# The opening of a fused layer-norm and linear-attention kernel: two steps listed by hand on every engine, norms of the weights taken over partitions by TensorE

## The reference

```python
q = (x @ Wq.T).reshape(B, L, H, D)
k = (x @ Wk.T).reshape(B, L, H, D)
v = (x @ Wv.T).reshape(B, L, H, D)
phi_q = jax.nn.elu(q) + 1.0
phi_k = jax.nn.elu(k) + 1.0
...
S = S + pk_t[..., :, None] * v_t[..., None, :]
z = z + pk_t
num = jnp.einsum('bhd,bhde->bhe', pq_t, S)
den = jnp.sum(pq_t * z, axis=-1, keepdims=True) + EPS
...
return out @ Wo.T + bo
```

## Time and profile before

| what | value |
|---|---|
| median of 3 runs | 969.82 us (969.0 to 972.33) |
| the profiled execution | 969.87 us, its span 968.1 us |
| busy share of the span | PE 93%, DVE 85%, ACT 78%, POOL 74% |
| mean granted clock of PE | 0.97 |

### The profile page before, as it was taken

One profiled execution on the slowest core, in us unless ns is written; L12 is line 12 of the kernel. 1 busy time (PEld: TensorE's weight loads), 2 busy tenths in 40 slices (PEclk: granted clock), 3 DMA queues, 4 the chain that ended last, 5 costly groups with the idle time before them and its releaser, 6 DMA issues. The chain is left out here.

```text
span 968.1 us, 29903 instructions
## 1 busy us (share of the span) xinstructions
PE 898.7 (93%) x10240; PEld 524.6 (54%) x10240; DVE 825.5 (85%) x1513; ACT 759.3 (78%) x1327; POOL 713.2 (74%) x879
## 2 busy tenths in 40 slices
PE   1368999999999999999999999999999999999974
PEld 1134555565555556655555556555555566555541
DVE  3376899998999999999999999999999999988763
ACT  4457888887888888888888888888888888878761
POOL 1036778777977777788877877788777777888761
PEclk8589999999999999999999999999999999999996
DMA  7136688787666877676767776776678776777772
GB/s 261 31 66 122 121 174 156 159 141 144 150 147 150 173 152 161 141 150 147 153 145 163 164 161 147 139 155 147 150 150 173 152 160 142 149 125 128 130 129 65
DMA packets 421404, 139.80 MB, mean 144 GB/s; under 512 B 402544, under 2 KB 402544, under 8 KB 421360
## 3 DMA queue, kind: packets, MB, share of 16 engines
q1 hardware_dynamic: 404496, 106.73, 59.4%
q10 hardware_dynamic: 16864, 32.51, 10.2%
HBM read 21.76 MB, written 16.78 MB: 40 GB/s over the span
## 5 line engine op out<-in xcount | busy, mean ns | idle before, releaser
L1125 PE MATMUL PJ<-wT,XT 128*128 128x512 f16 x2304 | 530.0, 382 | 15.4 <-DMA XT<-XH 7.6
L1125 PEld LDWEIGHTS PJ<-wT,XT 128*128 128x128 f16 x2304 | 217.7, 98 | 264.4 <-issue 18.0
L454 POOL TENSOR_TENSOR A<-AM,A 128x512 f16<-128x512 f32 x256 | 292.4, 1162 | 33.0 <-ACT A L649 33.0
L1224 PE MATMUL PJ<-wT,AT 128*128 128x512 f16 x768 | 178.5, 382 | 1.7 <-DMA AT<-ATTN 1.5
L446 POOL TENSOR_SCALAR_AFFINE_SELECT AM<-AM 128x512 f32<-128x512 f32 x128 | 81.8, 639 | 117.7 <-ACT AM L639 117.5
L649 ACT ACTIVATE A<-AM 128x512 f16<-128x512 f32 x256 | 153.9, 630 | 10.6 <-POOL AM L446 10.5
L1195 PE MATMUL AV<-SS,QS 128*128 128x33 f16 x1024 | 112.2, 178 | 5.4 <-POOL A L454 4.4
L1198 PE MATMUL AV<-VN,A 128*128 128x33 f16 x3072 | 116.9, 178 | 0.0
L1224 PEld LDWEIGHTS PJ<-wT,AT 128*128 128x128 f16 x768 | 71.7, 98 | 80.1 <-DMA AT<-ATTN 2.8
L1198 PEld LDWEIGHTS AV<-VN,A 128*128 128x128 f16 x3072 | 109.3, 96 | 3.7
L891 DVE TENSOR_TENSOR AM<-SC,causal 128x512 f32<-128x512 f32 x128 | 87.6, 684 | 22.9 <-PE SC L1175 22.7
(11 more groups left out here) (98 smaller groups left out, 1522.9 us busy)
## 6 DMA issues: line engine op xcount, KB each, us to landing
out_dram<-Y ACTq DMA_DIRECT2D x32, 512.0 KB, 3.1
X<-in_L_attn_x_dram ACTq DMA_DIRECT2D x30, 512.0 KB, 3.5
X<-in_L_attn_x_dram SPq DMA_DIRECT2D x2, 512.0 KB, 7.2
A<-in_L_attn_Wk_dram SPq DMA_DIRECT2D x1, 1024.0 KB, 9.4
A<-in_L_attn_Wq_dram SPq DMA_DIRECT2D x1, 1024.0 KB, 11.7
QS<-in_L_attn_Wv_dram SPq DMA_DIRECT2D x1, 1024.0 KB, 13.8
QS<-in_L_attn_Wo_dram SPq DMA_DIRECT2D x1, 1024.0 KB, 15.8
XT<-XH SPq DMA_TRANSPOSE x64, 3.5
```

The lines of the kernel that those rows point to most:

```text
L454: g.tensor_tensor(A[:, b, LO, hg], AM[:, k % 4], A[:, b, HI, hg], ALU.subtract).then_inc(a_lo.sem, 1)
L1125: ins = t_.matmul(PJ[b], XT[:, w, c, b * C:(b + 1) * C], wT[m_][:, m, c, :], start=(c, w, m) == todo[0], stop=(c, w, m) == todo[-1])
L1224: ins = t_.matmul(PJ[b], AT[:, b, w, c * C:(c + 1) * C], wT[3][:, m, c, :], start=(c, w, m) == todo[0], stop=(c, w, m) == todo[-1])
```

## The change

The loop and the end of the kernel keep their operations and their order. What is changed lies before step 1:

1. Every engine gets a function `opening()` that lists the preparation, step -1 and step 0 together, one operation a line; `run` begins at step 1. In it the squares, turned blocks and halves of the weights stand singly (a quarter of a weight at a time) between the operations of the chunks.
2. The maximum over partitions is no longer POOL's. For each weight PE turns the column of 128 partial maxima into one row (`turn_norm`), DVE reduces the row (`top_norm`), PE spreads the one number to all partitions by a matmul with a row of ones (`spread_norm`), and DVE makes the scale from it (`scale_w`, three linked instructions). The square root becomes a shift of the exponent bits by one place. The other scales come in `scale_rest`.
3. `gain` and `shift` have a semaphore each. DVE waits for the gain alone ahead of the first statistics and halves the shift after them (`half_gain`, `half_shift`). POOL and PE no longer wait for `zeroed`.
4. `NORMS` takes one of the PSUM banks, so that three spare banks serve the turned blocks instead of four; `W_REUSE` is 5 instead of 6.
5. `turn_q` waits in its first two steps for the high halves (`wT_hi`) of the weights that lie in the memory it writes.
6. The helper `wait(...)` becomes `wait_ge(*signal.upto(...))`, with the same counts.

```diff
-        W_BANKS = PJ + (SC + [AV2[:, i] for i in range(2)]) * 3 + SC
-        W_REUSE = len(PJ + SC) + 2
+        NORMS = AV2[:, 0]
+        spare = [SC[0], SC[1], AV2[:, 1]]
+        W_BANKS = PJ + [spare[k % 3] for k in range(4 * GROUPS - 2)]
+        W_REUSE = len(PJ + spare)
...
-            for s in range(-1, 4):
+            for s in range(1, 4):
...
+                        else:
+                            sp.wait_ge(wT_hi, (4 if ATTEND else 3) * GROUPS)
...
-            pool.wait_ge(zeroed, 1)
...
-                g.partition_all_reduce(norm2_all[:, at], norm2[:, at], P, RMAX).then_inc(norm2_reduced, 1)
-                pool.wait_ge(norm2_reduced, pair + 1)
-                g.tensor_tensor(norm[:, at], norm2_all[:, at], half4[:, at], ALU.pow).then_inc(norm_done, 1)
...
+            def row_sums(j):
+
+                m = W_ORDER[j]
+                dve.wait_ge(w_summed, (j + 1) * GROUPS)
+                link(v.tensor_reduce(norm2[:, m:m + 1], sumsq[:, m], mybir.AxisListType.X, ALU.max))
+                v.tensor_scalar(norm2[:, m:m + 1], norm2[:, m:m + 1], 1e-30, None, ALU.max).then_inc(norm2_done, 1)
+
+            def top_norm(j):
+
+                dve.wait_ge(norm_turned, j + 1)
+                v.tensor_reduce(norm_max[:, j:j + 1], NORMS[0:1, j * P:(j + 1) * P], mybir.AxisListType.X, ALU.max).then_inc(norm_max_done, 1)
+
+            def scale_w(j):
...
+                link(v.tensor_scalar(pow2[:, at].bitcast(U32), NORMS[:, j * P:j * P + 1].bitcast(U32), 1, EXP_BITS,
+                                     ALU.logical_shift_right, ALU.bitwise_and))
                 link(v.reciprocal(rpow2[:, at], pow2[:, at]))
...
+                v.tensor_scalar(w_scale[:, at], rpow2[:, at], TOP / HALF_EXP, None, ALU.mult).then_inc(w_scaled, 1)
+                dve.wait_ge(w_scaled, j + 1)
...
+            def turn_norm(j):
+
+                m = W_ORDER[j]
+                pe.wait_ge(norm2_done, j + 1)
+                t_.transpose(NORMS[0:1, j * P:(j + 1) * P], norm2[:, m:m + 1], ident[:]).then_inc(norm_turned, 1)
+
+            def spread_norm(j):
+
+                pe.wait_ge(norm_max_done, j + 1)
+                t_.matmul(NORMS[:, j * P:j * P + 1], ones_row[:], norm_max[:, j:j + 1], start=True, stop=True).then_inc(norm_spread, 1)
```

The first part of PE's new list and of ACT's (`early` is step -2, `first` step -1, `second` step 0):

```diff
+                w_turn(0, 0)
+                w_turn(0, 1)
+                turn_norm(0)
+                spread_norm(0)
+                w_turn(0, 2)
+                w_turn(0, 3)
+                turn_norm(1)
+                spread_norm(1)
+                w_turn(1, 0)
+                w_turn(1, 1)
+                w_turn(1, 2)
+                first.project_k(0)
+                turn_norm(2)
+                w_turn(1, 3)
+                w_turn(2, 0)
+                w_turn(2, 1)
+                spread_norm(2)
+                first.project_k(1)
+                first.project_q(0)
...
+                early.front_scale(0)
+                early.front_scale(1)
+                square(0, 0)
+                early.next_x()
+                square(0, 1)
+                square(0, 2)
+                square(0, 3)
+                square(1, 0)
+                square(1, 1)
+                early.normalise(0)
+                square(1, 2)
+                square(1, 3)
+                early.x_half(0)
+                w_half(0, 0)
+                w_half(0, 1)
+                w_half(0, 2)
+                w_half(0, 3)
+                early.normalise(1)
...
+                w_half(1, 3)
+                first.exp_relu_k(0)
+                square(3, 0)
```

## The result

| | before | changed |
|---|---|---|
| median of 4 runs | 970.42 us (969.0 to 972.33) | 940.67 us (940.12 to 942.95) |
| ratio, with its interval | | 0.9697 [0.9673, 0.9721] |
| the profiled execution, its span | 969.87, 968.1 us | 940.58, 938.8 us |
| mean granted clock of PE | 0.97 | 0.987 |

What follows compares the result with a forecast made beforehand. PE alone bounds the loop at 27.58 us a chunk, so only its entry can move: 91.54 to 62.4, 29.1 us, less 1.5 for clock and 1.5 for handovers, leaves 26.1; from 969.87 that gives 943.8 us, range 938 to 955.

Steps and rivals of the forecast that it cites:

- the mark: Start of `project_q(1)` of chunk 1, 91.54 us in the old kernel, forecast at 62.4, 29.1 earlier before deductions.
- Part 1: Opening up to the first projection: `project_k(0)` to start at 24.6 us against 42.07, 17.5 us earlier.
- The lost bank at 1.3 us: Before `project_k(0)`: with a bank fewer, PE's `w_turn(1, 1)` and `(1, 2)` wait for low halves, costing 1.3 us.
- Part 2: From the first projection to the last weight: ACT sets the pace, `v_half(1)` ends at 50.7 to 51.3 us.
- Part 3: Step 0 to `project_q(1)` of chunk 1: `scores(0, 0)` at 50.9, `project_k(1)` ends at 57.4, then 4.96 us to 62.4.
- The clock, 1.5 us, and the handovers, 1.5 us: Deductions before chunk 1: 1.5 us for half a second low-clock start, 1.5 for uncounted handovers, 3.0 off 29.1.
- All behind it should shift by as much: Behind `project_q(1)` of chunk 1: the loop, 27.58 us a chunk, forgets its entry, so everything later moves equally.
- the phase of the loop: Rival, 31 later chunks: another entry phase keeps a recurring PE wait, 0.84 us a chunk to break even; chance 0.05.
- Only the two reductions go: Rival, opening: interleaved lists give nothing beyond removing 2 x 7.1 us of POOL's waits, 955.6 us; chance 0.08.
- The slow route: Rival, weight norms: TensorE's route takes POOL's 8.4 us, Wk's scale comes 5.1 us late, 949 us; chance 0.04.
- The clock stays low: Rival, projections before chunk 1 at 1.2 GHz: throughout 958 to 960 us, chance 0.03; in part 947 to 953, 0.16.
- A second table load: ACT's opening: a load chosen for Identity might need another for Exp, 1.3 us more, giving 945 us.

Runs made afterwards that it cites:

- old_order: Changed kernel's TensorE norms in the old kernel's lists, with whole weights and `run` from step -1: 963.83 us, 0.9939 of the kernel before.
- k_first: Changed kernel with `project_k(0)` ahead of `w_turn(1, 1)` and `w_turn(1, 2)`: 943.61 us, 0.9746 of the kernel before.
- no_squares: Changed kernel without Wo's four squares on ACT, Wv's norm standing in: 940.75 us, 0.9711 of the kernel before.
- no_low: Changed kernel without Wo's four low halves on DVE: 941.32 us, 0.9719 of the kernel before.
- whole: Changed kernel with all four quarters of a weight standing together in every list: 953.81 us, 0.9838 of the kernel before.
- whole_but_pe: Changed kernel with whole weights in the lists of DVE and ACT, PE's list kept: 947.37 us, 0.9779 of the kernel before.
- pool_norm: Changed kernel with POOL's reduction over partitions put back, two weights at a time, new lists kept: 954.79 us, 0.9849 of the kernel before.
- no_both: Changed kernel without Wo's four squares on ACT and its four low halves on DVE: 939.14 us, 0.9689 of the kernel before.

## Why the prediction was right, and where it was not

- **The place of the gain** was right: 28.0 of 29.3 us lie ahead of the mark. Counted for it were 29.1. Part of any such difference is chance: the first square, which waits for Wk, starts at 11.72 us in the profiled execution of the old kernel and at 9.87 in old_order, whose opening begins alike.
- **Part 1** held row by row: the scale of Wk at 16.88 us (16.9), ACT at its first high half at 18.71 (19.1), `project_k(0)` at 24.27 (24.6). TensorE's route costs 1.4 us with its handovers (1.1 was taken, 1.0 to 1.6 were the bounds), and the cover that was to hide it is there: ACT wants the scale 1.8 us after it is ready. The rule of "GPSIMD Engine Reference" in the Trainium skill, that GpSimd is the only option for such a reduction, is not borne out: TensorE and DVE do it here, in 1.4 us against 8.4.
- **The lost bank at 1.3 us**: the wait is there (1.13 us, row 22.53), but what the bank is worth stays open. The turned quarters stand ahead of the projection for ACT's sake; k_first, which takes the projection out of this wait, loses 1.9.
- **Part 2, "ACT sets the pace"**, gave the right times (`v_half(1)` ends at 50.57 for 50.7 to 51.3; the last low half of Wo at 50.28 for 50.9) from half a cause. ACT's list was followed rightly: it has two holes there, 0.97 and 1.64 us, for the three of 1.4, 0.8 and 1.2 that were counted. But three microseconds fewer on ACT move nothing, because PE's projection holds it at the same place. And `scores(0, 0)` starts at 50.87, for 50.9, by luck: the prediction has it wait for the last low half of Wo, which was done at 50.28, and what it waited for is the first turn of k, landed at 50.8, which the prediction didn't count. no_squares and no_low show it.
- **Part 3**: `project_k(1)` ends at 58.56 (57.4), held 1.0 us by its turn. The prediction named `turn_k(1)`, issued at 51.6 and landed by 56.8, and found the turns in time. It took the landing times and not the time that SP is held by each issue: `turn_k(1)` is issued at 53.86, and the one that held PE was `turn_x(1)`, issued at 52.45 behind the others in the queue of SP. From there to the mark it is 4.96 us, as in the old kernel: 63.52 for 62.4.
- **The clock, 1.5 us, and the handovers, 1.5 us**: this term was mis-sized. The one slow start that the count had with 1.5 us came (`project_k(0)`, 4.14 us for 2.75, at a granted clock that the profile gives as 1.00); the one added to it did not. Of the 3.0 us subtracted 1.1 are real, and 1.0 of them is the wait for the turn.
- **"All behind it should shift by as much"** failed by 1.3 us. By DVE's quotients the distance of the two kernels grows from 28.0 us in chunk 1 to 28.3 in chunk 4, and by 1.0 in chunk 5, the one with the late turn shown above. The step that failed is "it forgets at once how it was entered", read from one chunk of 27.58: the next ones of the old kernel take up to 28.74, and only behind chunk 5 do all kernels take the same. old_order loses as much in these chunks as the old kernel, which speaks for the old entry and against the chance of one execution. That the phase of the loop matters was a rival, with the opposite sign.
- **The forecast of 26.1** is short by 3.6 of the medians' 29.7: 1.9 of the 3.0 taken off, 1.3 behind the mark, and 0.4 between the span and the medians. The 1.5 us for handovers came from no row.
- **Rivals.** "Only the two reductions go" (955.6) fell: both parts together give more than their sum. "The slow route" foresaw the first of its waits to 0.3 us (4.86) and would have been 949; it came out at 954.8, since the 7.2 us for which POOL stands behind each reduction weren't counted. "The clock stays low" fell in the changed kernel, and whole and whole_but_pe show that it was near: single waits of 2.7 to 4.0 us bring the granted clock down to 0.50. "A second table load" didn't come: ACT's timeline has one `ACT_TABLE_LOAD`, at 6.65 us, ahead of the first `rstd`. So "ScalarE: Activation LUTs" in the Trainium skill, with its anchor for each set, is not contradicted, but the load for Identity served for Exp as well.

## What to carry to other kernels

Where a start-up chain waits on one slow instruction and stands in the wrong order too, mend both before judging either: here they gave 5 and 14 us alone and 28 together. Before naming the engine that sets the pace, take work from it: here 3 us less on ACT and 2.3 us less on DVE moved nothing, since the first was hidden behind PE's projection and the second behind a transfer. Where the profile names an engine that had been done for some time, look at the landing of the transfers. When the preparation of weights is put between other work, cut it into pieces: whole weights cost 13 us here, because PE stood for banks, and one such wait of 2.7 us (row 52.22) cost 2.3 us more at the low clock.

## What the runs showed of the hardware

- A maximum over partitions by a turned column (0.37 us), a reduction of one row (0.28) and a spread by a row of ones (0.58 for the pair of matmuls, 0.38 later) takes 1.41 us with handovers for the first weight, and 1.42 to 1.43 for each of the four in old_order. POOL's own reduction lasts 0.37 us, and POOL stands idle around it. Behind it these are 7.13 and 7.07 us in the old kernel and 7.22 in pool_norm, and 7.19 counted from when the next instruction's data were ready; ahead of it 6.63 in pool_norm, 4.0 of them with the data there. It pays this at the second reduction as at the first. What POOL does in the gap the rows don't show.
- SP issues one transpose at a time: 1.23 us for `XT`, 1.77 to 3.54 us for `QS` and `KS` in the rows shown. At the start the queue's order is a resource like an engine. From issue to landing one and the same turn of k took 7.1, 7.7, 7.8 and 5.2 us in four kernels that issue it at the same place.
- The granted clock fell to 0.50 during PE waits of 2.72, 3.21 and 4.00 us and not during one of 0.99. In no_both it was 1.00 behind one of 2.60 (row 52.26).
- Before PE has run fast for the first time, its matmuls take as long as at 0.50 (twelve in 5.07 us in whole) while the profile gives a granted clock of 1.00. At the very start the durations are to be read and not that row.
- The first transfers land at times that differ by up to 1.9 us between executions. The opening goes with the gain's landing (12.56 us to the first high half in ten kernels), and a trace of a change worth 1 us must be read from there.
